# Pair 1's x transposes and q moved into the expert banks and beside pair 0's softmax, with the two fill rounds written out by hand

## What is computed

```python
# x (64, 256, 256), ctx (64, 77, 256), 4 heads of 64
q = rms_norm(layernorm(x) @ Wq, per head)
k, v = split(ctx @ Wkv); k = rms_norm(k, per head)
attn = softmax(q k^T / 8) v
x = x + tanh(g_xattn) * (attn @ Wfc + fc_b)
h = layernorm(x)
logits = h @ Wr^T                       # 8 experts
top_vals, top_idx = top_k(logits, 2); w = softmax(top_vals)
# every expert takes at most 97 tokens of a sequence, in order; later ones are dropped
x = x + tanh(g_ffn) * sum_k w_k * (h @ We[top_idx_k]) * kept
```

## Time and profile before

| what | us |
|---|---|
| median of 3 runs | 1443.17 (1442.71, 1443.17, 1445.39) |
| the profiled execution | 1446.5 |
| its span, first to last instruction | 1444.8 |
| busy: PE, PEld | 1401.2 (97%), 1177.1 (81%) |
| busy: DVE, ACT, POOL | 1111.4 (77%), 929.7 (64%), 766.2 (53%) |
| mean granted PE clock | 0.984 of full speed |

### The profile page before, as it was taken

How to read it: one execution, slowest core, us unless ns; L and a number is a source line. 1 busy time by engine, 2 the same in 40 slices (tenths; PEclk the granted TensorE clock), 3 DMA queues, 4 the chain that set the end, 5 groups by cost and what they waited for, 6 DMA issues and landing times. The chain is left out here.

```text
span 1444.8 us, 27347 instructions
## 1 busy us (share of the span) xinstructions
PE 1401.2 (97%) x8448; PEld 1177.1 (81%) x8448; DVE 1111.4 (77%) x3146; ACT 929.7 (64%) x2600; POOL 766.2 (53%) x915
## 2 busy tenths in 40 slices
PE   4789999999999999999999999999999999999998
PEld 3678888888888888888888888888888888888876
DVE  5668877778778778878778878778878778878763
ACT  6566676666676666676666676666676666676652
POOL 3325655555655555655545665545655545665544
PEclk8779999999999999999999999999999999999999
DMA  4001101001001011101011100010101010001000
GB/s 149 1 20 35 35 9 34 28 35 35 34 9 35 28 34 35 35 9 35 27 35 35 35 8 35 27 35 35 35 8 35 28 34 35 35 9 35 8 23 23
DMA packets 29075, 43.65 MB, mean 30 GB/s; under 512 B 4673, under 2 KB 12289, under 8 KB 28929
## 3 DMA queue, kind: packets, MB, share of 16 engines
q1 hardware_dynamic: 28928, 41.90, 8.5%
HBM read 25.11 MB, written 16.78 MB: 29 GB/s over the span
## 5 line engine op out<-in xcount | busy, mean ns | idle before, releaser
L310 PE MATMUL bkM<-we,x2T 128*128 128x512 f32 x3072 | 790.0, 398 | 5.5 <-ACT a_out L614 2.7
L310 PEld LDWEIGHTS bkM<-we,x2T 128*128 128x128 f32 x3072 | 552.5, 188 | 134.8 <-ACT a_out L614 17.9
L614 ACT ACTIVATE a_out<-bkM,gate 128x256 f32<-128x256 f32 x512 | 215.2, 476 | 164.8 <-PE bkM L310 160.3
L451 POOL TENSOR_TENSOR a_sum<-a_sum,a_out 128x256 f32<-128x256 f32 x256 | 188.2, 735 | 94.7 <-ACT a_out L614 62.9
L956 DVE SCALAR_TENSOR_TENSOR acc_v<-bkM,gate,acc_v 128x256 f32<-128x256 f32 x384 | 185.5, 483 | 56.0 <-PE bkM L310 46.9
L407 POOL TENSOR_TENSOR rstd<-ve,minus_half 128x4 f32<-128x4 f32 x64 | 64.8, 1012 | 221.6 <-DVE ve L751 221.6
L407 POOL TENSOR_TENSOR q_r<-q_ve,minus_half 128x16 f32<-128x16 f32 x32 | 93.1, 2911 | 119.1 <-DVE q_ve L835 119.1
L438 POOL TENSOR_TENSOR probs<-probs,p_inv 128x308 f32<-128x308 f32 x128 | 91.6, 715 | 77.8 <-DVE p_inv L850 77.8
L407 POOL TENSOR_TENSOR k_r<-k_ve,minus_half 77x8 f32<-77x8 f32 x32 | 52.2, 1632 | 139.7 <-DVE k_ve L800 139.7
L519 ACT ACTIVATE xn<-x_sb,shift,rstd 128x256 f32<-128x256 f32 x128 | 66.6, 591 | 80.1 <-DVE shift L760 80.1
L456 POOL TENSOR_TENSOR y<-a_sum,acc_v 128x256 f32<-128x256 f32 x128 | 94.4, 738 | 17.2 <-issue 0.4
(11 more groups left out here) (165 smaller groups left out, 2887.2 us busy)
## 6 DMA issues: line engine op xcount, KB each, us to landing
x_sb<-in_x SPq DMA_DIRECT2D x32, 512.0 KB, 3.9
out<-y SPq DMA_DIRECT2D x64, 256.0 KB, 2.0
ctx_sb<-in_ctx SPq DMA_DIRECT2D x32, 154.0 KB
stage<-in_L_ffn_We SPq DMA_DIRECT2D x2, 1024.0 KB, 7.8
stage<-in_L_xattn_Wkv SPq DMA_DIRECT2D x1, 512.0 KB, 5.3
stage<-in_L_xattn_Wq SPq DMA_DIRECT2D x1, 256.0 KB, 5.5
stage<-in_L_xattn_Wfc SPq DMA_DIRECT2D x1, 256.0 KB, 4.1
bias_bc<-in_L_xattn_fc_b SPq DMA_DIRECT2D x1, 128.0 KB, 5.5
```

Source lines behind the costliest of these rows:

```text
L310: mm = nc.tensor.matmul(out, l, r, start=(i == 0), stop=(i == len(terms) - 1))
L451: nc.gpsimd.tensor_tensor(a, o[:, 0] if i == 1 else a, o[:, i], ALU.add).then_inc(a_summed.sem, 1)
L614: ins = nc.scalar.activation(a_out[:, t % 2, (e // 4) * 2 + i], bkM[1][:, i * D:(i + 1) * D], ACT.Copy, scale=gate[:, m.parity, t, e:e + 1])
```

## The change

Pair 1's front uses bkM0 and bkM1 for the x transposes, q and q's transposes; all other pairs use bkA and bkB as before. The two rounds of the fill are no longer two calls of the slots. Round one (`first_round`) calls the slots of pair 0 and puts other work between them: pair 1's first layer norm on all engines, its x transposes ahead of pair 0's probability transposes, its xT split, and the context transposes at the end; xn of pair 0 comes between the conversions of wkv and wq, and wq, the tanh, wfc, wr and the first We half have other places. Round two (`second_round`) is a plain list: on PE q, kv, kv, fc, fc, q; the second layer norm's transposes; scores and logits; the probability transposes ahead of the positions. The second We half is converted in round two. `make_xb` runs after q's root in round two. DVE's `q_mean` has one more wait, in every step too. `x_transpose` of pair 1 does not wait for pair 0's residual. What was read from `xT_bank[k]` and `q_bank[i]` is now read from `front_bank(f, k)` and `front_bank(f, i)`. The diff, cut, by engines:

```diff
-        xT_bank = [bkA, bkB]
-        q_bank = [bkA, bkB]
+        front_banks = [bkA, bkB]
+        front_banks_in_fill = [bkM[0], bkM[1]]
...
-        def qT_half(i):
-            return q_bank[i][:].rearrange("p (m c) -> p m c", m=KC)
+        def front_bank(f, i):
+            return (front_banks_in_fill if f.n == 1 else front_banks)[i]
+        def qT_half(f, i):
+            return front_bank(f, i)[:].rearrange("p (m c) -> p m c", m=KC)
```

POOL (the old fill was two calls of `slots`; the `fill` of every engine now calls the two rounds):

```diff
+            def first_round(f, g):
+                ln1(f)
+                k_rsqrt(f)
+                make_xb(f, 0)
+                ln1(g)
+                q_rsqrt(f)
+                for t in (1, 3, 2):
+                    make_xb(f, t)
+                for t in range(T):
+                    normalise(f, t)
+            def second_round(p, f):
+                k_rsqrt(f)
+                ln2(p)
+                q_rsqrt(f)
+                for t in range(T):
+                    make_xb(f, t)
+                for t in range(T):
+                    normalise(f, t)
             def fill():
-                slots(None, None, Pair(0, 0))
-                slots(None, Pair(0, 0), Pair(0, 1))
+                first_round(Pair(0, 0), Pair(0, 1))
+                second_round(Pair(0, 0), Pair(0, 1))
```

ACT:

```diff
                 if k == 3:
                     if f:
-                        ln1(f)
+                        if not xn_made:
+                            ln1(f)
                         kv(f, 0)
...
+            def first_round(f, g):
+                for k in range(SLOTS):
+                    if k == 3:
+                        weights_hi([0])
+                        ln1(f)
+                        weights_hi([1])
+                    slot(k, None, None, f, xn_made=True)
+                    if k == 4:
+                        gates()
+                        weights_hi(range(UNGATED, FRONT_WEIGHTS))
+                    if k == 8:
+                        ln1(g)
+                        weights_hi([FRONT_WEIGHTS])
+                    if k == 13:
+                        xT_part(g, 0)
+                        xT_part(g, 1)
+            def second_round(p, f):
+                o_part(p, 1)
+                ctx_hi(f)
+                q(f, 0)
+                kv(f, 0)
+                kv(f, 1)
+                weights_hi([FRONT_WEIGHTS + 1])
+                q(f, 1)
+                q_part(f, 0)
+                k_part(f)
+                q_part(f, 1)
+                ln2(p)
+                x2T_part(p, 0)
+                x2T_part(p, 1)
+                exps(f, 0)
+                logits(p)
+                exps(f, 1)
+                exps(f, 2)
+                exps(f, 3)
+                router_exp(p)
+                for t in range(T):
+                    pT_part(f, t)
+                o_part(f, 0)
```

DVE:

```diff
                 dve.wait_ge(q_r_done.sem, q_r_done.before(f))
+                dve.wait_ge(exp_done.sem, exp_done.before(f))
...
                 if k == 14:
...
-                    if f:
+                    if f and f.n > 0:
                         pT_part(f, 2)
                         pT_part(f, 3)
...
+            def first_round(f, g):
+                for k in range(SLOTS):
+                    slot(k, None, None, f)
+                    if k == 2:
+                        weights_lo(range(UNGATED))
+                    if k == 4:
+                        gated_constants()
+                        weights_lo(range(UNGATED, FRONT_WEIGHTS))
+                    if k == 5:
+                        ln1(g)
+                    if k == 8:
+                        ln1_shift(g)
+                    if k == 10:
+                        weights_lo([FRONT_WEIGHTS])
+                    if k == 13:
+                        pT_part(f, 2)
+                        pT_part(f, 3)
+                        xT_part(g, 0)
+                        xT_part(g, 1)
+            def second_round(p, f):
+                o_part(p, 1)
+                ctx_lo(f)
+                q_sums(f, 0)
+                kv(f, 0)
+                kv(f, 1)
+                residual(p, 0)
+                residual(p, 1)
+                k_scale(f)
+                q_sums(f, 1)
+                q_mean(f)
+                ln2_shift(p)
+                q(f, 0)
+                k_part(f)
+                q(f, 1)
+                weights_lo([FRONT_WEIGHTS + 1])
+                x2T_part(p, 0)
+                x2T_part(p, 1)
+                row_max(f, 0)
+                row_max(f, 1)
+                route(p, 0)
+                row_max(f, 2)
+                inverse(f, 0)
+                row_max(f, 3)
+                route(p, 1)
+                inverse(f, 1)
+                inverse(f, 2)
+                inverse(f, 3)
+                gates(p)
+                for t in range(T):
+                    pT_part(f, t)
+                kept_gates(p)
+                o_part(f, 0)
```

PE (the waits for `stage_used` and `setup_v` stood in the old fill at the same slots, that for all front weights ahead of slot 0 of round two):

```diff
-                pe.wait_ge(x1_done.sem, x1_done.before(f))
+                if f.n != 1:
+                    pe.wait_ge(x1_done.sem, x1_done.before(f))
...
+            def first_round(f, g):
+                for k in range(SLOTS):
+                    if k == 2:
+                        pe.wait_ge(stage_used, 1)
+                        pe.wait_ge(setup_v, ZEROS)
+                    if k == 5:
+                        pe.wait_ge(stage_used, 2)
+                    if k == 6:
+                        pe.wait_ge(setup_v, SETUP_V)
+                    if k == 13:
+                        x_transpose(g)
+                    slot(k, None, None, f)
+                ctx_transpose(g)
+            def second_round(p, f):
+                q(f, 0)
+                kv(f, 0)
+                kv(f, 1)
+                pe.wait_ge(stage_used, FRONT_WEIGHTS)
+                fc(p, 0)
+                fc(p, 1)
+                q(f, 1)
+                q_transpose(f, 0)
+                k_transpose(f)
+                q_transpose(f, 1)
+                x2_transpose(p, 0)
+                x2_transpose(p, 1)
+                scores(f, 0)
+                logits(p)
+                scores(f, 1)
+                logits_transpose(p)
+                scores(f, 2)
+                scores(f, 3)
+                for t in range(T):
+                    p_transpose(f, t)
+                positions(p)
+                attend(f, 0, 0, p)
+                attend(f, 0, 1, p)
+                attend(f, 1, 0, p)
+                attend(f, 1, 1, p)
```

More of the change, by code:

```diff
@@ L538, in xT_part @@
                 act.wait_ge(q_ps.sem, q_ps.before(f))
-                copy(xT[:, 0, k], xT_bank[k][:]).then_inc(xT_hi.sem, 1)
+                copy(xT[:, 0, k], front_bank(f, k)[:]).then_inc(xT_hi.sem, 1)
             def kv(f, b):
@@ L551, in q @@
                 act.wait_ge(q_ss_done.sem, q_ss_done.before(f))
-                nc.scalar.activation(q_sq[:, i], q_bank[i][:], ACT.Square).then_inc(q_sq_done.sem, 1)
+                nc.scalar.activation(q_sq[:, i], front_bank(f, i)[:], ACT.Square).then_inc(q_sq_done.sem, 1)
                 act.wait_ge(xT_ps.sem, xT_ps.at(f))
-                copy(q_nat[:, 2 * i:2 * i + 2], q_bank[i][:].rearrange("p (t d) -> p t d", d=D)
+                copy(q_nat[:, 2 * i:2 * i + 2], front_bank(f, i)[:].rearrange("p (t d) -> p t d", d=D)
                      ).then_inc(q_nat_done.sem, 1)
@@ L559, in q_part @@
                 act.wait_ge(s_ps.sem, s_ps.before(f))
[L560 removed]
+                copy(qT[:, 0, :, i * LQ:(i + 1) * LQ], qT_half(f, i)).then_inc(q_hi.sem, 1)
             def k_part(f):
@@ L692, in slot @@
                         o_part(f, 0)
-            def fill():
-                for f, p in ((Pair(0, 0), None), (Pair(0, 1), Pair(0, 0))):
-                    for k in range(SLOTS):
-                        slot(k, None, p, f)
-                        if k == 2 and p is None:
-                            weights_hi(range(UNGATED))
-                            gates()
-                            weights_hi(range(UNGATED, FRONT_WEIGHTS))
-                        if k in (7, 8) and p is None:
-                            weights_hi([FRONT_WEIGHTS + k - 7])
+            def first_round(f, g):
[37 more added lines that the diff above has]
+                o_part(f, 0)
+            def fill():
+                first_round(Pair(0, 0), Pair(0, 1))
+                second_round(Pair(0, 0), Pair(0, 1))
             def step(m, p, f, ahead):
@@ L822, in q @@
                 half = slice(i * LQ, (i + 1) * LQ)
-                lo(qT[:, 1, :, half], qT_half(i), qT[:, 0, :, half]).then_inc(q_lo.sem, 1)
+                lo(qT[:, 1, :, half], qT_half(f, i), qT[:, 0, :, half]).then_inc(q_lo.sem, 1)
             def q_sums(f, i):
@@ L1053, in slot @@
                         o_part(f, 0)
-            def fill():
-                for f, p in ((Pair(0, 0), None), (Pair(0, 1), Pair(0, 0))):
-                    for k in range(SLOTS):
-                        slot(k, None, p, f)
-                        if k == 2 and p is None:
-                            weights_lo(range(UNGATED))
```

(6 more changed lines are left out.)

27 lines of the change are left out of this document (9 added, 18 removed).

## The result

The changed kernel takes 1435.51 us (four runs, 1435.02 to 1435.99), the kernel before beside it 1444.21; the ratio is 0.9936, with a 95% interval of 0.9923 to 0.9949. I had forecast 3.1, and the time lies 2.1 us under the lower end of the range. The profiled execution took 1435.99 us with a span of 1434.3, 10.5 less than before.

What follows compares the result with a forecast made beforehand. TensorE was taken to bound the loop and a latency chain the two-round fill, whose savings come off one for one. Round one 2.6 plus round two 0.5 made 3.1 us off 1443.17: 1440.1 us, range 1437.6 to 1443.3.

Steps and rivals of the forecast that it cites:

- What bounds it: TensorE bounds the loop, a latency chain walked twice the fill; only what the fill's two rounds save shortens the span.
- (a): Round one, start: xn of pair 0 right behind wkv's conversion; transposes 1.5 us earlier, at 12.77, q at 15.5.
- (b): Round one, DVE: pair 1's layer-norm statistics take 2.0 us behind k's scaling; POOL's power counted at nothing (bounds 0 and 1.0).
- (e): Round one: pair 1's eight x transposes, between last scores and first probability transpose, cost nothing on the path.
- (f): Round one: the clock may fall before the second q half (2.8 us, not 1.7), costing 1.5 us with its transposes.
- (c): Round one, ACT: second qT copy ahead of We conversions; first exponential at about 29.2 instead of 30.23, 1.0 us saved.
- (d): Round one: We low part moved off the fourth normalising product, which takes 0.70 us instead of 2.71; 2.0 us saved.
- the sum with the early fall: Round one's total saving if the clock falls before the second q half: 1.6 to 2.0 us.
- the line of six: Round two, TensorE: q, kv, kv, fc, fc, q; ends at 54.4 or 56.0 us by when the clock rises.
- Everything fits: Rival: no early clock fall, high clock through round two's scores; saves 3.3, then 1.9 plus 0.4: 1437.6 us; chance 0.20.
- The slower one: Rival: clock stays low through round two's six products, ending at 60.6; 1446.5 us taken; chance 0.06.
- signs of being wrong: Loop length from second attention's end moved by over 0.5 us, or round one's first exponential past 30.6.

Runs made afterwards that it cites:

- e4: Changed kernel with round two's two fc products put ahead of pair 1's q and kv: 1441.44 us, ratio 0.9989 to the kernel before.
- e5: Changed kernel with DVE's first We low part put back behind the fourth inverse in round one: 1443.51 us, ratio 0.9993 to the kernel before.
- e13: Changed kernel itself, measured again on another chip: 1437.05 us, ratio 0.9953 to the kernel before.
- e11: Changed kernel with the first We low part moved out of round one's softmax to round two: 1442.73 us, ratio 0.9985 to the kernel before.
- e2: Changed kernel with the added wait in q_mean kept for pair 1 alone: 1436.11 us, ratio 0.9949 to the kernel before.
- e9: Kernel before with only DVE's low part of the second We half moved from behind the fourth inverse to behind the second: 1443.62 us, ratio 0.9980.
- e3: Kernel before with only the added wait in q_mean: 1445.30 us, ratio 1.0007.

## Why the prediction was wrong

**What bounds it** held in the main: the gain came off the fill and, against "nothing else of the change can", 1.3 us off the first step behind it, by the clock. Later steps moved by nothing that is the change's.

**Round one** came out at 43.76 for 44.0, but for another reason than the sum's. (a) x transposes at 12.93 for 12.8, q at 16.00 for 15.5. (b) and (e) cost nothing, as said. (f) happened: the clock fell at 20.5, the second q half took 2.77 us, and the first exponential came at 30.73, where (c) with (f) had 30.6. (d) was over-sized. The low part did move off the last product, onto the second: it ran on DVE from 34.11 to 36.43, and the second, third and fourth products together took 4.03 us from 34.27. The last ended at 38.3, 1.4 us earlier than before. But the last transpose came only 0.9 us earlier than in the earlier trace rows (38.83 for 39.75), because the last three now stood behind one another at the low clock; with the first exponential 0.5 us later, (d) was worth 1.4 us and not 2.0. So up to the last transpose the sum with the early fall, 1.6 us, came out at 0.9, and the 2.6 that I took was 1.7 too much. Against that stand 1.9 us of the attention at the high clock, which the sum did not have. Two errors of nearly 2 us cancelled; the 44.0 was luck.

**Round two** is where it failed, in the sentence that the clock rises "at 47.3" or "at 50.7". It had risen at 41, so the line of six ended at 52.8 where I had 54.4 or 56.0. From there to the first exponential I had 10.0 or 9.9 us, and it took 10.0; the low clock for x2's transposes and scores was forecast rightly. From the first exponential to the end I had 17.3 and it took 15.5: 1.9 us is the attention at the high clock (3.7 for 5.6). After that the first step's products ran at the high clock too, 2.9 us from the attention's end to fc where it had been 4.2; I had no term for that. So the 8.5 us up to the loop are 2.8 of round one, 4.4 of round two and 1.3 behind it, and I had 2.6, 0.5 and nothing.

**The order** was under-valued as well, by the same step: with the clock high, fc first costs 2.0 us (e4), and my 0.5 was a difference between a line at the low clock and rows at the high one.

**The step behind it.** I took from the earlier trace rows how long after a product the clock had risen in one execution, and put that delay behind the first dense products of round two. I did not ask what else in the new order would be dense. By the Trainium skill (TensorE: Matmul & The Clock Gate, "What's actually happening") activity lifts the clock; I used this for round two's line, and the trace agrees, only the activity came earlier: the bunched transposes from 37.05 on and the first 1.3 us of the attention. It agrees less in round two of the kernel before, where TensorE worked from 76.0 on with no gap over 0.1 us and the clock came up at 88.1. By the Trainium skill (SBUF — State Buffer, "Who interferes with whom") the low part and POOL's product exclude each other; 2.32 us against 4.03 us for three products agree. The rule told where the lock went, not that it would be useful there.

**The rivals.** "Everything fits" was nearest in direction, but counted a high clock from the scores on, not from the attention. The slower one, a low clock through the line of six, came in no profile: even in e5, which loses nearly all of the gain, the clock was back at 49.5 us. That one execution had the clock's history and another might not was in the text only as a reason for the baseline, and should have been a rival. In the end the early rise is not certain either: e13 has two runs in six without the gain's larger part, if their 1441 to 1442 us are of this kind; their mean clock points that way, and no profile caught one.

**The signs.** Two of the signs of being wrong came, both for other reasons than the text gave. The first exponential of round one was past 30.6, at 30.73, by the early fall. And the loop's length, from the end of the second attention, moved by 3.3 us (1359.3 to 1356.0): 1.3 by the clock in the first step, 1.9 by the length of a step, which differs among executions of one kernel.

## What to carry to other kernels

In a fill or any stage that is bound by latency, go through TensorE's stretches of the new order and ask which level of the clock each will have, before pricing them; one instruction of another engine that spreads or bunches TensorE's work can be worth more than the work moved. A stall that is shared with other work may bunch what follows it, so look at what comes behind it before removing it. And take the level and the steps' length from several executions: here one kernel's runs lay 7 us apart.

## What the runs showed of the hardware

- One DVE instruction of 2.32 us, moved by two slots, changed the median by 6 to 8 us (e5 0.9993; the changed kernel 0.9936 and 0.9953), in e5's profile mostly by way of the granted clock; taking it out of the softmax cost 5 to 7 (e11 0.9985, in which 1.8 us are its own place in round two).
- The four probability transposes, bunched, were followed by a rise of the clock after 2.9 to 4.0 us (round two of the changed kernel, e2, e13, e9, e11) or only after 12 (the kernel before, e4, e5).
- The kernel before ran from 1440.7 to 1449.8 us in all. Its profiles have round one's attention end at 46.6, 48.8 and (e3, with the wait that does nothing) 49.7 us, and the clock's records begin at 13.0, 18.6 and 20.0 us in them. In the earlier trace rows the first six kv products take 2.84 us, nearly twice the 1.6 of the later ones, in a stretch for which the windows give 1.00 (9.6 to 13.0 us): ahead of the first record that column is no measurement.
- A step of the loop took 43.27 or 43.35 us in one and the same kernel (after, e13), with 1 or 18 waits of TensorE for ACT, 0.4 or 3.2 us in all.
